# A fused transformer kernel: keys and values of two context attentions made in earlier loops and kept in DRAM

## What is computed

```python
x = block0(x, ctx)   # attention 0 (self, causal, window 64, distance bias), norm,
                     # attention 1 (on ctx), norm, feed-forward with gelu, norm
x = block1(x, ctx)   # attention 2 (self, causal), norm, attention 3 (on ctx), norm, feed-forward, norm
x = block2(x, ctx)   # q = norm(x) Wq;  k, v = norm(ctx) Wkv:  attention 4;  x + o;  x + feed-forward with silu
x = block3(x, ctx)   # attention 5, k and v from ctx;  norm(x + o)
# one attention, per head:
s = q @ k.T * scale;  a = softmax(s);  o = a @ v;  out = o @ Wo + bo
# feed-forward: act(x @ W1 + b1) @ W2 + b2, with 1024 hidden columns
```

## Time and profile before

| | us |
|---|---|
| median of 3 runs (3622.07 to 3624.68) | 3624.45 |
| the profiled execution, device time | 3608.98 |
| its span, first to last instruction | 3607.2 |
| PE busy in it | 3413.1 |
| DVE busy in it | 2452.5 |
| ACT busy in it | 2117.0 |

### The profile page before, as it was taken

One profiled execution on the slowest core, in us unless ns is written; L12 is line 12 of the kernel. 1 busy time (PEld: TensorE's weight loads), 2 busy tenths in 40 slices (PEclk: granted clock), 3 DMA queues, 4 the chain that ended last, 5 costly groups with the idle time before them and its releaser, 6 DMA issues.

```text
span 3607.2 us, 54314 instructions
## 1 busy us (share of the span) xinstructions
PE 3413.1 (95%) x19508; PEld 1519.3 (42%) x19508; DVE 2452.5 (68%) x3819; ACT 2117.0 (59%) x3767; POOL 544.7 (15%) x473
## 2 busy tenths in 40 slices
PE   7899999999989999999999999999999999999997
PEld 5434434433444443443344454344335345344332
DVE  3675687666776577766678658776577865866666
ACT  1465565566646556666555655656674665665665
POOL 2111211101220111111032111111012111201101
PEclk8999999999999999999999999999999999999999
DMA  6311321122221231122232022112233212212121
GB/s 221 107 48 54 108 76 54 66 68 99 91 88 45 77 107 57 54 77 66 92 116 86 29 89 93 51 57 77 78 101 99 93 54 80 73 48 70 57 65 42
DMA packets 285471, 280.57 MB, mean 78 GB/s; under 512 B 50434, under 2 KB 276610, under 8 KB 281218
## 3 DMA queue, kind: packets, MB, share of 16 engines
q1 hardware_dynamic: 258324, 274.74, 23.2%
q10 hardware_dynamic: 26880, 2.37, 0.6%
HBM read 195.74 MB, written 81.26 MB: 77 GB/s over the span
## 4 chain that ended last, share of the span: by engine, by line
PE 80%; DVE 12%; ACT 3%; issue 3%; DMA 0%; POOL 0%; ACTq 0%; SPq 0%; DVEq 0%; POOLq 0%
PE pv L777 15%; PE st L751 14%; PE mx L826 10%; PE mx L690 9%; PE st L788 9%; DVE row_max L963 7%; PE mx L720 7%; PE st L701 4%; PE mx L798 4%; ACT probs L887 3%; PE mx L823 2%; DVE y L1031 2%; PE st L756 1%; PE st L836 1%; PE mx L728 1%
## 5 line engine op out<-in xcount | busy, mean ns | idle before, releaser
L887 ACT ACTIVATE probs<-st 128x512 f32<-128x512 f32 (+1 forms) x2624 | 1378.0, 589 | 865.8 <-PE st L751 509.8
L963 DVE TENSOR_REDUCE row_max<-mx 128x2 bf16<-128x1024 f32 (+3 forms) x1536 | 1525.1, 1037 | 452.6 <-PE mx L720 264.0
L751 PE MATMUL st<-q_packed,k_packed 97*128 97x512 bf16 (+2 forms) x3072 | 858.1, 352 | 41.3 <-ACT probs L887 28.4
L777 PE MATMUL pv<-probs,va 128*32 128x512 f32 (+2 forms) x6144 | 710.5, 536 | 9.7 <-ACT probs L887 8.7
L751 PEld LDWEIGHTS st<-q_packed,k_packed 97*128 97x128 bf16 (+1 forms) x3072 | 253.9, 98 | 708.2 <-ACT probs L887 394.6
L720 PE MATMUL mx<-k_high,qm 32*128 32x512 bf16 (+2 forms) x3072 | 368.6, 352 | 63.4 <-DVE row_max L963 47.7
L788 PE MATMUL st<-xT,w1s 128*128 128x512 f32 x768 | 361.8, 606 | 0.0
L1081 POOL TENSOR_TENSOR rstd<-spread_of,m_half 128x2 f32<-128x2 f32 x144 | 100.2, 696 | 1580.1 <-DVE spread_of L1025 1579.7
L720 PEld LDWEIGHTS mx<-k_high,qm 32*128 32x128 bf16 x3072 | 109.9, 91 | 452.7 <-issue 235.9
L1068 POOL TENSOR_TENSOR qm<-q_high,own_rows 128x512 bf16<-128x512 bf16 x192 | 198.6, 1045 | 555.3 <-ACT q_high L850 555.3
L1006 DVE TENSOR_TENSOR y<-mx,row 128x512 f32<-128x512 f32 x112 | 77.3, 690 | 260.2 <-PE mx L826 257.4
(11 more groups left out here) (88 smaller groups left out, 3159.4 us busy)
## 6 DMA issues: line engine op xcount, KB each, us to landing
k_packed<-k_parts_dram SPq DMA_DIRECT2D x576, 128.0 KB, 2.6
q_packed<-q_parts_dram SPq DMA_DIRECT2D x576, 128.0 KB, 2.6
q_parts_dram<-q_low SPq DMA_DIRECT2D x96, 256.0 KB, 2.5
k_parts_dram<-k_low SPq DMA_DIRECT2D x96, 256.0 KB, 2.1
q_parts_dram<-q_high SPq DMA_DIRECT2D x48, 256.0 KB, 2.1
k_parts_dram<-k_high SPq DMA_DIRECT2D x48, 256.0 KB, 2.1
w1s<-w_dram SPq DMA_DIRECT2D x12, 1024.0 KB, 4.9
w2s<-w_dram SPq DMA_DIRECT2D x12, 1024.0 KB, 7.2
```

What stands on the lines that cost most here:

```text
L751: mm = pe.matmul(bank[:, m * w:(m + 1) * w], packed["k"][contracted, h, k * P:(k + 1) * P], packed["q"][contracted, h, q0:q1], start=(m == ...
L777: mm = pe.matmul(pv[j * PAIR:(j + 1) * PAIR, q0:q1], va[s][:, k, at:at + PAIR], probs[:, step % 2, c:c + q1 - q0], start=(k == 0 and k_kin ...
L887: act.activation(probs[:, step % 2, e * TOK:e * TOK + w], held["scores", b, a, n, e][:, 0:w], ACT.Exp, scale=ATT_SCALE[a]) \
L963: dve.tensor_reduce(row_max[s][:, c:c + TT + 1:TT], held["max", b, a, g, i][half][:, :, 0:k1 - k0], AX_X, ALU.max, negate=True).then_inc(* ...
```

## The change

Keys and values of attentions 4 and 5, and the normalization of the context, are made in other loops: `EARLY` names them. Loop 01 makes those of attention 5 for slot 0, loop 10 the same for slot 1, loop 21 those of attention 4 for slot 0 with the normalization, loop 30 the same for slot 1. Before, they were made in 41, 50, 31 and 40. The high part of the keys goes to `early_high`, values to `early_va`, and both to DRAM. A new stage `fetch`, in the loop where the keys were made before, brings them back into `k_high` and `va`. `ncT` now lies in the last two tiles of `hid`. The slots in DRAM for key parts are three times as many. PE waits for `high_back` and `va_back` where it waited for ACT's copies. The table `MERGE` has new strings for every kind of loop but the last; of its strings one stands here.

```diff
+EARLY = {"01": (0, 5), "10": (1, 5), "21": (0, 4), "30": (1, 4)}
...
 def context_stages(b, a):
+    if early(a):
+        yield "fetch", b, a
+    else:
+        yield from project_stages(b, a, "k")
+        yield "middle", b, a, "k"
+    for w in HML:
+        yield "load", b, a, 0, "k", w
+    if not early(a):
+        yield from value_stages(b, a)
+    if a == 4:
+        yield "next_context", b
+
+def early_stages(b, a):
     if a == 4:
         yield from norm_stages(b, "ctx")
     yield from project_stages(b, a, "k")
     yield "middle", b, a, "k"
-    for w in HML:
-        yield "load", b, a, 0, "k", w
     yield from value_stages(b, a)
-    if a == 5:
-        yield "next_context", b
...
+    if f"{a}{b % SLOTS}" in EARLY:
+        s, then = EARLY[f"{a}{b % SLOTS}"]
+        context += early_stages(b // SLOTS * SLOTS + s, then)
...
-    "01": "011001023032202220010011011012013010220100001120001300102010011002200001320200232002220000002000"
-           "00002030220023",
+    "01": "011001230003222220010010111001021012323031000010021010210100022000010000002102301222220302300200"
+           "0000202000233333000",
...
+        early_high = sb("early_high", [P, KT, TOK], BF16)
+        early_va = sb("early_va", [P, TT, VROW])
-        ncT = sb("ncT", [P, KT, TOK])
+        ncT = hid[:, FT - KT:FT]
...
+                elif kind == "project_v" and early(stage[2]) and stage[3]:
+                    a = stage[2]
+                    sp.wait_ge(*st_drained.past(("v", b, a, 1)))
+                    sp.dma_start(v_dram[a - 4, b % SLOTS], early_va[:]).then_inc(early_v_out, 16)
+                elif kind == "fetch":
+                    a = stage[2]
+                    two_before = LOOPS[LOOP_NO[b, a] - SLOTS]
+                    sp.wait_ge(*part_sent(b, a, "k", "h"))
+                    sp.wait_ge(*max_filled.past(("max", *two_before, NG - 1, TT - 1, 1)))
+                    sp.dma_start(high["k"][b % SLOTS][:], parts_of(b, a, "k")[0].rearrange("(t p) n -> p t n", p=P)) \
+                        .then_inc(high_back, 16)
+                    sp.wait_ge(early_v_out, 16 * (early_no(b, a) + 1))
+                    sp.wait_ge(*step_done.past(("values", *two_before, STEPS - 1)))
+                    sp.dma_start(va[b % SLOTS][:], v_dram[a - 4, b % SLOTS]).then_inc(va_back, 16)
...
-                            pe.wait_ge(*act_step.past(("h", b, a, "k", t)))
+                            pe.wait_ge(*((high_back, 16 * (fetch_no(b, a) + 1)) if early(a) else act_step.past(("h", b, a, "k", t))))
...
-                        pe.wait_ge(*st_drained.past(("v", b, a, 1)))
+                        pe.wait_ge(*((va_back, 16 * (fetch_no(b, a) + 1)) if early(a) else st_drained.past(("v", b, a, 1))))
...
+                    if m == "k" and early(a) and t == 0 and early_no(b, a):
+                        act.wait_ge(early_out["h"], 16 * early_no(b, a))
...
+                    if early(a) and not half and early_no(b, a):
+                        act.wait_ge(early_v_out, 16 * early_no(b, a))
...
+            for values in (*va, early_va):
+                nc.gpsimd.memset(values[:], 0.0)
```

More of the change, by code:

```diff
@@ L41, with early, early_no, fetch_no @@
 NORM = {"a0": 0, "a1": 1, "f0": 2, "a2": 3, "a3": 4, "f1": 5, "pre": 6, "a5": 7, "ctx": 8}
+EARLY = {"01": (0, 5), "10": (1, 5), "21": (0, 4), "30": (1, 4)}
 FFN_INPUT = {0: "a1", 1: "a3", 2: "a4"}
 Q_INPUT = {1: "a0", 2: "f0", 3: "a2", 4: "pre", 5: "f2"}
+def early(a):
+    return a > 3
+def early_no(b, a):
+    return b // SLOTS * len(EARLY) + list(EARLY.values()).index((b % SLOTS, a))
+def fetch_no(b, a):
+    return b // SLOTS * len(EARLY) + (a - 4) * SLOTS + b % SLOTS
+def k_slot(b, a):
+    return b % SLOTS + (SLOTS * (a - 3) if early(a) else 0)
+def k_rank(b, a):
+    return sum(not early(x) for _, x in LOOPS[:LOOP_NO[b, a]])
 def own(a):
@@ L336 @@
 PLAN = list(plan())
+K_MADE = [(b, a) for kind, b, a, m, *_ in (stage for stage in PLAN if stage[0] == "middle") if m == "k"]
+K_BEFORE = dict(zip(K_MADE[1:], K_MADE))
 class Signal:
@@ L440, in bias, with high_of, staged, parts_of @@
             return 0.0 if a == 4 else cv(f"b{m}{a}")[:, t:t + 1]
-        def staged(b, m, w):
-            return high[m][b % SLOTS][:] if w == "h" else low[m][:, HML.index(w) - 1]
+        def high_of(b, a, m):
+            return early_high if m == "k" and early(a) else high[m][b % SLOTS]
+        def staged(b, a, m, w):
+            return high_of(b, a, m)[:] if w == "h" else low[m][:, HML.index(w) - 1]
+        def parts_of(b, a, m):
+            return in_dram[m][k_slot(b, a) if m == "k" else b % SLOTS]
+        def part_sent(b, a, m, w):
+            if m == "k" and early(a):
+                return early_out[w], 16 * (early_no(b, a) + 1)
+            return part_out[m, w], 16 * ((LOOP_NO[b, a] if m == "q" else k_rank(b, a)) + 1)
+        def made_before(b, a, m):
+            return before(b, a) if m == "q" else K_BEFORE.get((b, a))
         def target(b, tag):
```

90 lines of the change are left out of this document (48 added, 42 removed).

## The result

The changed kernel takes 3636.41 us (median of 6 runs, 3633.07 to 3637.07), the kernel before 3620.5 us (6 runs, 3614.89 to 3624.68). The ratio is 1.0042, with an interval of 1.0029 to 1.0055: slower by 0.4%, 15 us. The forecast was 3609 us, 15 us faster. The time lies in the range of 3562 to 3654, on the side that had a chance of 0.25.

What follows compares the result with a forecast made beforehand. PE, busy 95% of the span, was taken as the bound. Fill -36, clock -8, waits gone -8, fillers gone +8 and cover lost +29 made -15 us, so 3624.45-15 = 3609 us, range 3562 to 3654.

Steps and rivals of the forecast that it cites:

- fillers gone: Loops 31, 40, 41, 50: value projections no longer stand between attention steps, so PE idles more; +8 us in the run.
- Waits filled in the receiving loops: Loops 01, 10, 21, 30: moved work fills PE's waits; -36 us in the run, bounds 0 and 68.
- The clock: Start of loop 30, clock 0.54 over 11.1 us: projections placed ahead restore it; -8 us, at most 11.
- The 20 us of the price by the Trainium skill: Start of loop 30: throttled time priced by one minus the granted share, 5.1 us, 20 in the run; not adopted.
- Waits gone from the giving loops: Loop 31: the normalization's waits of 1.41 and 0.57 us go with its instructions; -8 us in the run.
- The fetches: Values and keys brought back from DRAM, issued a loop ahead and so hidden: 0 us; 78 if uncovered.
- the rival of a late fetch: Fetches of values and keys come late and show: up to +78 us, 3687 us; chance 0.02.
- rival 4: Loops 21 and 30: DVE replaces PE as bound through the normalization; +59 us, 3683, half of it 3654; chance 0.12.
- Its sign: Deciding sign of rival 4: waits for row_max in loops 21 and 30 grow rather than shrink.
- The cover lost at the start of 40, 41 and 50: Output projection there waits for oT without a key projection or normalization ahead: 2.1, 2.6, 2.96 us; +29 in the run.
- rival 3: New clock falls of 2 us each in loops 31, 40, 41, 50, start of 30 unrepaired: +25, 3649 us; chance 0.10.
- New order elsewhere: Other loops get other orders of the same instructions; counted 0, with 20 us either way.

Runs made afterwards that it cites:

- e6: Changed kernel, but attention 5 of slot 1 is not made early (loops 10 and 50 as before): ratio 0.9994 to the kernel before, 3617.15 us.
- e9: Kernel before with attention 4 and the normalization alone made early, plus the changed kernel's orders in first, 00, 11, 20, 51; no useless matmuls: ratio 0.9935, 3598.10 us.
- e1: Kernel before, with attention 5's key projection in loops 41 and 50 put behind attention 4's output projection instead of ahead: ratio 1.0120, 3658.43 us.
- e2: Changed kernel plus three useless matmuls at the end of loops 31, 40 and 41: ratio 1.0004 to the kernel before, 3615.87 us.
- e4: Changed kernel with the orders of before in the first loop and 00, 11, 20, 51: ratio 1.0074 to the kernel before, 3642.41 us.
- e3: Kernel before with only attention 4's keys, values and normalization made early (loops 21 and 30), without the new orders elsewhere: ratio 0.9969, 3606.10 us.
- e10: e9 with keys and values of attention 5, slot 0, made in loop 40 instead of 41: ratio 0.9931 to the kernel before, 3598.75 us.
- e7: e6 plus three useless matmuls at each of the borders 11/20, 31/40 and 40/41: ratio 0.9952 to the kernel before, 3603.12 us.
- e5: Kernel before plus three useless matmuls at the end of loop 11: ratio 0.9987, 3613.99 us.

## Why the prediction was wrong

By the profiles, over four pairs, with 143.2 us of PE work moved:

| | forecast | measured |
|---|---|---|
| receiving loops, beyond the work: fill and clock | -44 | +96.8-143.2 = -46.4 |
| giving loops, beyond the work: waits gone, fillers gone, cover lost | -8+8+29 = +29 | -61.2+143.2 = +82.0 |
| other loops, up to the first score and elsewhere | 0 | -5.9-4.4 = -10.3 |
| all | -15 | +25.3 |

What lies beyond the work can be taken apart further, with the idle time of PE (length less busy) and the clock's sums:

| | idle | clock | rest | all |
|---|---|---|---|---|
| receiving loops | 47.2-67.8 = -20.6 | 17.0-25.5 = -8.5 | -17.3 | -46.4 |
| giving loops | 78.0-38.9 = +39.1 | 36.8-11.6 = +25.2 | +17.7 | +82.0 |

*Waits filled in the receiving loops: right in sum, and that is luck.* The waits gave 20.6 us, not 36. Idle in loop 01 fell to 44.20-42.71 = 1.5 us, with 1 forecast. In 10 and 21 it did not fall (3.9 and 4.0 us, where 1.5 and 1.8 were to be left); in 30 it fell from 6.0 to 2.6. The clock gave 8.5 us, and 17.3 us lie in PE's busy time, which grew by less than the work that came and the clock account for. The giving loops have a rest of the same size with the other sign, so the moved work may simply have weighed less than 143.2 us; what these rests are is not shown. The fill is uneven: over the four pairs, 01 and 10 took both shares of attention 5 (60.8 us of work) for 36.7 us, and slot 0's alone, in e6, for 29.6 of 30.4. Against e9, which shares the other new orders, these are 31.1 and 24.0 us. So most of what was hidden there was slot 1's.

*The clock: right in sum, wrong in place.* At the start of 30 it is 0.54 over 11.1 us before and after in the pair shown, and over the four pairs 3.4 of 18.7 us came back, where 8 were forecast. The projections ahead of it did not hold the clock. Another 5.1 of 6.8 us came back around the end of 01, where the forecast expected nothing; whether that shortened the loop, with DVE busy there, no run shows. The 20 us of the price by the Trainium skill, "TensorE: Matmul & The Clock Gate", Terms, did not come either, since little was repaired.

*Waits gone from the giving loops: right.* The waits of the normalization at the end of 31 went with it. *The fetches: right.* Values go and come in transfers of 574.0 KB that land in 3.6 and 4.5 us, and neither is a releaser of PE anywhere, so the rival of a late fetch is out. *DVE in 21 and 30: not the bound.* By rival 4 the receiving loops would have lost the fill and 38 us more; they are 46.4 us shorter than work alone would make them. Its sign did not come either: in 21 and 30 of each pair PE waited 3.5 us for row_max before and 2.6 to 3.3 us after.

*The cover lost at the start of 40, 41 and 50: the step that failed.* The wait was right as a mechanism and was named; its size was 29 us, and that was all the price it had. The giving loops got 39.1 us more idle time and lost 25.2 us more by the clock, where +29 us in all was forecast for them. Three things were mis-sized or left out.
- The maxima do not cover. I took 0.4 us off for one group of them and 0.85 for maxima and scores. Maxima are emptied by DVE, the engine whose chain was being waited for. At 40/41 DVE's two reductions stand behind `oT`:

```profile
1613.24 0.71 DVE L1079 STREAM_TRANSPOSE oT<-normal 128x512 f32<-128x512 f32 x1
1613.88 2.32 DVE L1048 TENSOR_REDUCE row_max<-mx 128x2 bf16<-128x1024 f32 x2
```

  `oT` is ready at 1613.95, but the output projection writes into a pair of `mx` that the first reduction has to read, and it starts at 1615.21, 1.3 us later. At 41/50, with nothing between, it starts 0.06 us behind `oT`. So with maxima between, PE waits 3.89 us at 31/40 and 3.29+1.16 us at 40/41, and with nothing between 2.96 at 41/50. The sum is 11.3 us in this pair where 7.7 was forecast, and 43 us against 31 over the four pairs (29 with loop 20's share).
- The clock behind the wait. The sum had no term for it, and it took 25.2 us more: 17.0 at 40/41, 5.1 at 41/50, 3.4 at 31/40. The output projection of attention 4 alone is 15.9 us slower. This is rival 3's mechanism in places that it did not name: it gave a new fall of 2 us to each giving loop, 32 us, for want of fillers at their ends, while the falls stand behind the new waits. Its +25 us for the whole meets the 25.3 us of the profiles only because other terms cancel.
- The rest of the 82 us. 43 of new waits and -8 of normalization waits are 35 of the 39.1 us of idle time, so at most some 4 are left for *fillers gone*, forecast at 8. The 17.7 us in PE's busy time that the clock doesn't account for are not assigned.

e1 shows the wait and the clock without any of the other parts of the change (+43 us at eight borders), and e2 shows that covering with work of no other value gives back 14 us. That is less than the 41 us of the group row: at 41/50 such work leaves the 2.96 us as they are and only holds the clock, and at 40/41 a wait of another kind remains.

*New order elsewhere: counted 0, worth -12 us* (e4, and e9 against e3). It lay in my allowance of 20 either way. Without it the change would have been 0.74% slower.

What stays open: why e10's useful cover brings nothing in all, though it shortens the wait that it was put under and the clock takes 8 us less; what ends the waits of scores that the profile calls "issue" at 31/40; and the two rests of 17 us above. For the second, the code has these scores wait also for the maxima's rows to come back from DRAM, a transfer that ScalarE issues at 1509.72 in e9, 2.4 us before they start. That would fit, but no run shows it alone.

## What to carry to other kernels

Before work is moved because other places have waits to fill, look at what it covers where it stands: a key projection between the last product and a chain on VectorE was worth 5.4 us there, and 3.7 us of work. Price such a wait twice, as idle time and, at worst, as matmuls at half clock behind it, and read the clock in every repetition of the place, not in one. Cover it with matmuls that the waited engine need not empty, and try a large move in parts: here half of it, attention 4, was a gain of 11 us, and the other half a loss of 38.

## What the runs showed of the hardware that I had not expected

The same wait did not always cost the clock. At 11/20 of the kernel before, PE waited 2.96 us, and the stretch behind it is:

```profile
1204.30:1209.00 4.70, 4.69 (x27) 3.93 (x28) 1.97 (x7) 0.00 (x0) 0.15 (x1) 1.00 0.67 204
```

All four pairs are like this. At 41/50 of the changed kernel the same 2.96 us are followed by a clock of 0.55 for 6.7 us in one pair and by slow matmuls for a part of the way in another, and in two by none. And at its border 11/20, where one group of maxima now stands between, PE waits 2.61 us, and the stretch behind is low in all four pairs:

```profile
1213.50:1219.50 6.00, 5.21 (x21) 4.23 (x22) 2.07 (x6) 0.00 (x0) 0.00 (x0) 0.72 0.63 196
```

The Trainium skill, "TensorE: Matmul & The Clock Gate", "Why this matters for your kernels", advises no gaps of over about 3 us; these waits, just under it, fell on both sides, and the shortest of them lost the clock each time. Nor is one long wait needed: the start of loop 30 has 0.54 over 11.1 us with 0.4 us idle in it (11.10-10.72), and what stands just ahead are two waits for maxima, of 1.32 and 0.74 us.

With three useless matmuls in the wait, the eight behind it took 3.70 us in every pair, where they had taken up to 6.67. A kernel became faster by doing more, 14 us in e2, 15 in e7, while in e5, where the clock had not fallen, the same matmuls brought 4 us at most.
